# A causal linear attention and feed-forward layer: the last tile's attention within its own slot, and work moved between queues

## The chip, the cores and the metric

The kernel runs on one core of one Trainium2 chip. The metric is the device time of one execution in microseconds (us), the median of several runs. TensorE is called PE below, VectorE DVE, ScalarE ACT, GpSimd POOL and SyncE's queue SP. A change of under 0.2% (4.7 us) is about what a measurement of this kernel can't tell from no change.

## What is computed

The input x is 8 x 2048 x 512 in float32. Per batch, with 16 heads of 32 features and LN for a layernorm without weights:

```python
q, k, v = heads(x @ Wq.T + bq), heads(x @ Wk.T + bk), heads(x @ Wv.T + bv)
q, k = exp(q), exp(k)
kv = cumsum(k[:, :, :, None] * v[:, :, None, :], axis=1)
k1 = cumsum(k, axis=1)
out = einsum('zsD,zsDd->zsd', q, kv) / sum(q * k1, axis=-1, keepdims=True)
x = LN(x + out @ Wo.T + bo)
x = LN(x + tanh(((x @ weight) @ aux_weight1) @ aux_weight2 + bias))
```

## The kernel before

The 2048 rows of each of the 8 batches are cut into 16 tiles of 128 rows, so there are 128 tiles. They are taken in an order in which neighbours belong to different batches: tile n is rows of batch n % 8. The weights are multiplied together and split once at the start, each into a high part (H, fp32r) and a rest (L), and a product of two such matrices takes three passes: H by H, L by H, H by L, over four blocks of 128 rows (`three_pass`, lines 312 to 314, 12 matmuls of 128x512).

All five engines run the same slots, one function `slot(c, k)` each, and slot k works on several tiles at once. The conditions `att` (tile k exists), `prev` (tile k - 1), `ffn` (tile k - 2), `fin` (tile k - 3) and `proj` (tile k + 4) say what is there. So a tile is spread over slots:

- Four slots or more ahead: its rows x are loaded (SP, L277), turned (DVE, L674), split (ACT L567, POOL L761), and Q and K are projected for four tiles at once (PE).
- Slot n: scores of tile n (PE, L410), copied from PSUM into A (ACT, L532), masked (POOL, L723); the running sum of K (DVE, L654) and its product with Q (L662); V projected (PE) and copied out (ACT, L562); the residual's rows loaded (SP, L296) and cbc, the bias after Wo, added to them on POOL (L754).
- Slot n + 1: denominators (PE, L393), the part from the state (L397), and A by V, called AV here (L419). Then o: a reciprocal (DVE, L684), a product (L686), oH (ACT, L542), oL (POOL, L734), the projection by Wo (PE), the sum with the residual (DVE, L700), the first layernorm's statistics (L702 and L704, POOL L765 to L770).
- Slot n + 2: x1, the first layernorm's result (ACT, L522), goes to DRAM and back (SP, L267 and L284) and is turned (DVE, L696) and split (ACT L546, POOL L748); the product with Wf (PE).
- Slot n + 3: bias (DVE, L648), tanh (ACT, L527), the sum with x1 (POOL, L730), statistics (DVE L689 and L692, POOL L738 to L743), the last scaling (ACT, L557), and the store (SP, L300).

Within a slot PE's order is: denominators and state part of tile k - 1, scores of tile k, AV of tile k - 1, state update, Q and K projections, V projection of tile k, Wo for tile k - 1, Wf for tile k - 2. The last slots are cut down: Q and K projections stop after slot 123; slots 124 to 127 are the last with scores, slot 128 has AV, Wo (tile 127) and Wf (tile 126), slot 129 has Wf (tile 127), and slot 130 only finishes tile 127.

Nothing is scheduled by a tool: the order on each engine is the order in which the functions are written, and each queue is taken strictly in order. The PSUM tile ND holds numerators and denominators, one set for all tiles, so those of the next tile can't be written until L686 has read the last ones (semaphore `o_ready`). The SBUF tiles o, oH and oL have one copy each too, as x1s, x1H and x1L. SC is shared: Wo's result lies in its fourth bank, V's in its third, and Q's and Wf's in its first.

```python
                if prev:
                    wait(dve, oproj_done, c.count(k))
                    wait(dve, xb_ready, c.count(k))
                    nc.vector.tensor_tensor(r, oproj_ps, r, ALU.add).then_inc(r_ready, 1)
```

These lines end DVE's slot (L697 to L700). `xb_ready` says that the residual has had its cbc added.

Of the kernel before, what the change touches and what calls it, by code (L numbers as in the profile page):

```python
# [26 lines left out]
def linear_attention_ffn_kernel(nc, x, wqT, wkT, wvT, woT, bq, bk, bv, bo, w, a1T, a2, bf, out):  # L27
    F32 = mybir.dt.float32
    F32R = mybir.dt.float32r
    ALU = mybir.AluOpType  # L30
# [26 lines left out]
    with ctx:  # L57
# [171 lines left out]
        def _(sp):  # L229
# [33 lines left out]
            def slot(c, k):  # L263
# [8 lines left out]
                if c.exists(k + 9):  # L272
                    n = k + 9

                    wait_before(sp, (xl_ready, c.count(n - 1)))
                    for j in range(HG):
                        sp.dma_start(xin[j * HD:(j + 1) * HD, n % XIN, :].rearrange("p (t f) -> p t f", t=HG),  # L277
                                     x_b[n % B, c.it + n // B, j]).then_inc(xin_loaded[n % B], 16)
# [7 lines left out]
                if c.updates_state(k - 1):  # L286
                    n = k - 1
                    wait_before(sp, (k_stored[n % B], c.dma_count(n)), (state_done, c.count(n)))
                    for j in range(HG):
                        sp.dma_start(Ktok[j * HD:(j + 1) * HD, :].rearrange("p (a c) -> p a c", a=HG),  # L290
                                     k_blocks[j]).then_inc(ktok_loaded[n % B], 16)
                if c.exists(k):
# [15 lines left out]
        def _(pe):  # L308
# [40 lines left out]
            def slot(c, k):  # L349
# [4 lines left out]
                pcols = slice((k - 1) % QUAD * P, ((k - 1) % QUAD + 1) * P)  # L354
                ps = ((k - 1) // QUAD) % 2
# [5 lines left out]
                         for g in range(NK) for j in range(HG)]  # L361

# [25 lines left out]
                if prev:  # L388

                    wait_before(pe, (qk1_ready, c.count(k)), (o_ready, c.count(k - 1)),  # L390
                                (state_ready, c.state_count(k - 2)))
                    for g, j, quarter, h in heads:
                        last = nc.tensor.matmul(den_ps[quarter, j, :], ones[h, :], qk1[h, g, :], start=True, stop=True)  # L393
                    last.then_inc(den_done, 1)
                    if c.reads_state(k - 1):
                        for g, j, quarter, h in heads:
                            nc.tensor.matmul(num_ps[quarter, j, :], state[h, (k - 1) % B, g, :], QT[h, ps, g, pcols],  # L397
                                             start=True, stop=False, skip_group_check=True)
# [14 lines left out]
                if prev:  # L413
                    wait(pe, v_ready, c.count(k))
                    wait(pe, masked, c.count(k))
                    for j in range(HG):
                        for g in range(NK):
# [392 lines left out]
```

## Time and profile before

| | us |
|---|---|
| median of 3 runs | 2340.22 |
| lowest and highest | 2339.27 and 2342.91 |
| the profiled execution's own time | 2341.11 |
| its span (first to last instruction) | 2339.2 |
| PE busy in the span | 2249.3 (96%) |
| DVE, ACT, POOL busy | 1494.7, 1004.2, 1415.9 |

The profile is of one execution. Its own time is 1.9 us longer than its span, and 0.9 us longer than the median. In rows of a timeline or a chain the first number is the start in us from the start of the span, and the second the duration in us. Matmuls overlap, so that a row's duration of 0.39 is longer than the step from one to the next, 0.23 at the full clock.

### The profile page before, as it was taken

Reading aid. Unit: us, or ns where it says so; the run is one execution under the profiler, and the core shown is the slowest. Engines: PE = TensorE matmul, PEld = TensorE weight load, DVE = VectorE, ACT = ScalarE, POOL = GpSimd, SP = SyncE. Lnnn points to the kernel's source line nnn. Section 1 sums busy time; section 2 is a strip of 40 time slices with the busy share of each in tenths; the row PEclk is TensorE's granted clock in tenths of the full one; section 3 lists DMA queues with packets and bytes.
Section 4 is the critical chain, followed back from the end, with each engine's and each line's share of the span. In section 5 each row is a group of like instructions: output and inputs, shape, how many; then the busy total and the mean of one; then the engine's idle time right before and its main releaser. Section 6 shows DMA issues by size and latency. Waiting matters only on the chain.

```text
span 2339.2 us, 71230 instructions
## 1 busy us (share of the span) xinstructions
PE 2249.3 (96%) x27784; PEld 1834.5 (78%) x27784; DVE 1494.7 (64%) x2316; ACT 1004.2 (43%) x1683; POOL 1415.9 (61%) x1925
## 2 busy tenths in 40 slices
PE   3999999999999999999999999999999999999985
PEld 2778888888888888888888888888888888878863
DVE  3466676666666766666667666676676666666653
ACT  2344444444444444444444444444444444444432
POOL 1256666666666666666666666666666666666563
PEclk9999999999999999999999999999999999999997
DMA  5133333333333333333333333333333333333221
GB/s 155 48 96 112 107 109 111 103 110 109 106 113 100 113 110 101 110 109 106 113 101 110 114 100 113 106 108 111 103 110 111 101 114 105 107 108 101 71 67 50
DMA packets 294452, 242.73 MB, mean 104 GB/s; under 512 B 33328, under 2 KB 225840, under 8 KB 294192
## 3 DMA queue, kind: packets, MB, share of 16 engines
q1 hardware_dynamic: 294192, 238.69, 32.6%
q8 instruction: 234, 3.83, 0.7%
q14 instruction: 26, 0.21, 0.0%
HBM read 139.99 MB, written 98.57 MB: 102 GB/s over the span
## 4 chain that ended last, share of the span: by engine, by line
PE 92%; DVE 2%; issue 2%; SPq 1%; DMA 1%; ACT 1%; POOL 1%; POOLq 0%; DVEq 0%; ACTq 0%
PE SC L312 25%; PE SC L313 24%; PE SC L314 24%; PE SC L410 6%; PE ND L419 5%; PE ND L397 3%; PE ND L393 2%; PE ND L429 2%; DVE o L684 1%; SPq L277 1%; DMA xres<-x 0%; PE ND L312 0%; PE ND L314 0%; DVE WK L654 0%; PE ND L313 0%
## 5 line engine op out<-in xcount | busy, mean ns | idle before, releaser
L723 POOL TENSOR_SCALAR_AFFINE_SELECT A<-A 128x512 f32<-128x512 f32 x512 | 329.3, 678 | 297.3 <-ACT A L532 297.2
L684 DVE RECIPROCAL o<-ND 128x512 f32<-128x512 f32 x128 | 427.8, 3342 | 1.6 <-PE ND L419 1.3
L700 DVE TENSOR_TENSOR xres<-SC,xres 128x512 f32<-128x512 f32 x128 | 88.5, 692 | 483.2 <-PE SC L314 358.0
L734 POOL TENSOR_TENSOR oL<-o,oH 128x512 fp32r<-128x512 f32 x128 | 165.3, 1291 | 325.0 <-ACT oH L542 325.0
L522 ACT ACTIVATE WK<-xres,shift,rstd 128x512 f32<-128x512 f32 x128 | 104.1, 813 | 501.5 <-POOL shift L770 501.5
L532 ACT ACTIVATE A<-SC 128x512 f32<-128x512 f32 x512 | 264.3, 602 | 36.0 <-PE SC L410 35.0
L312 PE MATMUL SC<-xTH,WqH 128*128 128x512 f32 x512 | 211.1, 412 | 32.3 <-POOL xTL L761 27.6
L312 PE MATMUL SC<-WoH,oH 128*128 128x512 f32 x512 | 202.4, 395 | 17.8 <-issue 16.5
L761 POOL TENSOR_TENSOR xTL<-xin,xTH 128x512 fp32r<-128x512 f32 x128 | 165.6, 1294 | 85.9 <-ACT xTH L567 85.9
L654 DVE TENSOR_TENSOR_SCAN WK<-ones,k,KT 128x128 f32<-128x128 f32 x512 | 207.6, 467 | 8.8 <-PE ND L393 8.3
L312 PE MATMUL SC<-WfH,x1H 128*128 128x512 f32 x512 | 201.0, 393 | 10.4 <-POOL x1L L748 9.4
L312 PE MATMUL SC<-xTH,WkH 128*128 128x512 f32 x512 | 199.9, 390 | 7.2 <-DVE WkL L596 7.2
L537 ACT ACTIVATE QT<-SC,bcol 128x512 f32<-128x512 f32 x128 | 88.3, 690 | 272.3 <-PE SC L314 272.3
L312 PE MATMUL SC<-WvH,xTH 128*128 128x512 f32 x512 | 199.6, 390 | 2.7 <-ACT A L532 2.7
L314 PE MATMUL SC<-WoH,oL 128*128 128x512 f32 x512 | 202.0, 394 | 0.0
L313 PE MATMUL SC<-WoL,oH 128*128 128x512 f32 x512 | 201.8, 394 | 0.0
L313 PE MATMUL SC<-xTL,WqH 128*128 128x512 f32 x512 | 200.8, 392 | 0.7 <-issue 0.3
L314 PE MATMUL SC<-xTH,WqL 128*128 128x512 f32 x512 | 201.4, 393 | 0.0
L313 PE MATMUL SC<-WfL,x1H 128*128 128x512 f32 x512 | 200.4, 391 | 0.0
L314 PE MATMUL SC<-WfH,x1L 128*128 128x512 f32 x512 | 199.9, 390 | 0.0
L313 PE MATMUL SC<-xTL,WkH 128*128 128x512 f32 x512 | 199.7, 390 | 0.0
L314 PE MATMUL SC<-xTH,WkL 128*128 128x512 f32 x512 | 199.6, 390 | 0.0
(100 smaller groups left out, 5006.0 us busy)
## 6 DMA issues: line engine op xcount, KB each, us to landing
xin<-x SPq DMA_DIRECT2D x512, 64.0 KB, 2.0
xres<-x SPq DMA_DIRECT2D x128, 256.0 KB, 2.6
x_rows<-WK SPq DMA_DIRECT2D x128, 256.0 KB, 2.6
WK<-x_rows SPq DMA_DIRECT2D x512, 64.0 KB, 1.9
out<-WK SPq DMA_DIRECT2D x128, 256.0 KB, 2.0
k_rows<-WK SPq DMA_DIRECT2D x120, 256.0 KB, 2.0
WK<-k_rows SPq DMA_DIRECT2D x480, 64.0 KB, 1.9
QT<-wqT SPq DMA_DIRECT2D x4, 256.0 KB, 4.8
```

Source lines behind the costliest of these rows:

```text
L312: nc.tensor.matmul(out, statH(k), movH(k), start=(k == 0), stop=False)
L313: nc.tensor.matmul(out, statH(k), movL(k), start=False, stop=False)
L314: last = nc.tensor.matmul(out, statL(k), movH(k), start=False, stop=(k == NK - 1))
L410: last = nc.tensor.matmul(SC[:, j, g * P:(g + 1) * P], KT[h, s, g, cols], QT[h, s, g, cols], start=True, stop=True)
L419: last = nc.tensor.matmul(num_ps[g * HD:(g + 1) * HD, j, :], V[:, (k - 1) % 2, f0:f0 + HD], A[:, (k - 1) % 2, j, g, :], start=not c.reads_ ...
L522: nc.scalar.activation(x1[:, n % 2, :], xres[:, n % 2, :], ACT.Identity, bias=shift[:, 0:1], scale=rstd[:, 0:1]).then_inc(x1_ready, 1)
L532: nc.scalar.activation(A[:, k % 2, j, :, :].rearrange("p g q -> p (g q)"), SC[:, j, :], ACT.Copy).then_inc(scores_out[j], 1)
L654: last = nc.vector.tensor_tensor_scan(qk1[:, g, :], ones[:, 0:1].to_broadcast([P, P]), KT[:, s, g, cols], k1[:, k % B, g:g + 1], ALU.mult, ...
L684: nc.vector.reciprocal(o[:, :, :], den_ps).then_inc(recip_ready, 1)
L723: last = nc.gpsimd.affine_select(out=A[:, k % 2, j, :, :], in_=A[:, k % 2, j, :, :], compare_op=ALU.is_ge, fill=0.0, base=0, pattern=[[0, ...
L734: nc.gpsimd.tensor_tensor(oL[:, :, :], o[:, :, :], oH[:, :, :].bitcast(F32), ALU.subtract).then_inc(ol_ready, 1)
L761: nc.gpsimd.tensor_tensor(halves[1], xin[:, m % XIN, :].rearrange("p (t g q) -> p g t q", t=HG, q=HD), halves[0].bitcast(F32), ALU.subtrac ...
```

## The change

On PE, DVE, ACT and POOL the steps of AV and o become functions of a tile number (`denominators`, `attend`, `normalise`, `split_o`, `rest_of_o`). They are called as before where tile k exists, and in the slot of the last tile (127) a second time, for tile 127 itself, so that slot 128 no longer has them. Besides:

- ACT copies V (`copy_v`) ahead of `split_o` where `proj` is false (slots 124 to 127); elsewhere it stays behind K's exponential. The last scaling of tile k - 3 moves behind the copy of V and the split of x.
- The addition of cbc to the residual moves from POOL to DVE, from the slot of tile k into that of tile k + 1, just ahead of the sum that uses it.
- SP issues the loads of x for tile k + 9 behind the two loads back from DRAM (x1 and K), not ahead of them.

```diff
@@ sync, slot
-                if c.exists(k + 9):
-                    n = k + 9
-
-                    wait_before(sp, (xl_ready, c.count(n - 1)))
-                    for j in range(HG):
-                        sp.dma_start(xin[...] ...)
                 if c.exists(k - 2):
...
                         sp.dma_start(Ktok[j * HD:(j + 1) * HD, :].rearrange("p (a c) -> p a c", a=HG),
                                      k_blocks[j]).then_inc(ktok_loaded[n % B], 16)
+                if c.exists(k + 9):
+                    n = k + 9
+
+                    wait_before(sp, (xl_ready, c.count(n - 1)))
+                    for j in range(HG):
+                        sp.dma_start(xin[...] ...)
@@ tensor, slot
+                def denominators(n):
+
+                    ts, tcols = (n // QUAD) % 2, slice(n % QUAD * P, (n % QUAD + 1) * P)
+
+                    wait_before(pe, (qk1_ready, c.count(n + 1)), (o_ready, c.count(n)),
+                                (state_ready, c.state_count(n - 1)))
...
+                def attend(n):
+                    wait(pe, v_ready, c.count(n + 1))
+                    wait(pe, masked, c.count(n + 1))
...
-                if prev:
...
+                if att and prev:
+                    denominators(k - 1)
                 if att:
...
-                if prev:
...
+                if att and prev:
+                    attend(k - 1)
...
                     three_pass(v_ps, ...).then_inc(v_done, 1)
+                if att and not c.exists(k + 1):
+                    denominators(k)
+                    attend(k)
                 if prev:
                     output_projection()
@@ scalar, slot
+                def split_o(n):
+                    wait(act, o_ready, c.count(n + 1))
+                    wait(act, oproj_done, c.count(n))
+                    nc.scalar.activation(oH[:, :, :], o[:, :, :], ACT.Copy).then_inc(oh_ready, 1)
+
+                def copy_v():
+                    wait(act, v_done, c.count(k + 1))
+                    wait(act, state_done, c.state_count(k - 1))
+                    nc.scalar.activation(V[:, k % 2, :], v_ps, ACT.Copy).then_inc(v_ready, 1)
...
-                if prev:
...
+                if att and not proj:
+                    copy_v()
+                if att and prev:
+                    split_o(k - 1)
...
-                if fin:
...
-                if att:
...
+                if att and proj:
+                    copy_v()
                 if c.exists(k + 8):
...
+                if fin:
...
+                if att and not c.exists(k + 1):
+                    split_o(k)
@@ vector, slot
+                def normalise(n):
+
+                    wait(dve, num_done, c.count(n + 1))
+                    wait(dve, oh_ready, c.count(n))
+                    wait(dve, ol_ready, c.count(n))
+                    nc.vector.reciprocal(o[:, :, :], den_ps).then_inc(recip_ready, 1)
...
-                if prev:
...
+                if att and prev:
+                    normalise(k - 1)
...
                     nc.vector.transpose(x1s[:, :], x1s[:, :]).then_inc(x1_turned, 1)
+                if att and not c.exists(k + 1):
+                    normalise(k)
                 if prev:
+                    wait(dve, xres_loaded[(k - 1) % B], c.dma_count(k - 1))
+                    nc.vector.tensor_tensor(r, r, cbc[:, :], ALU.add).then_inc(xb_ready, 1)
                     wait(dve, oproj_done, c.count(k))
@@ gpsimd, slot
-                if att:
-                    if not prev:
-                        pool.wait_ge(c_ready, 1)
-                    wait(pool, xres_loaded[k], c.dma_count(k))
-                    nc.gpsimd.tensor_tensor(xres[:, k % 2, :], xres[:, k % 2, :], cbc[:, :],
-                                            ALU.add).then_inc(xb_ready, 1)
...
+                if att and not c.exists(k + 1):
+                    rest_of_o(k)
                 if prev:
                     wait_before(pool, (stats1_ready, c.count(k)))
```

The engine orders at the places that matter. On PE, at the end of slot 127, before (L312 to L314 with Wv are V's projection, with Wo the output projection of tile 126):

```order
L312 MATMUL SC<-WvH,xTH 128x512
L313 MATMUL SC<-WvL,xTH 128x512
L314 MATMUL SC<-WvH,xTL 128x512
L312 MATMUL SC<-WoH,oH 128x512
L313 MATMUL SC<-WoL,oH 128x512
```

and in the changed kernel (L368, L372 and L381 are denominators, state part and AV, of tile 127):

```order
L312 MATMUL SC<-WvH,xTH 128x512
L313 MATMUL SC<-WvL,xTH 128x512
L314 MATMUL SC<-WvH,xTL 128x512
L368 MATMUL ND<-WK,ones 32x128 x16
L372 MATMUL ND<-QT,state 32x128 x16
L381 MATMUL ND<-A,V 32x128 x16
L312 MATMUL SC<-WoH,oH 128x512
L313 MATMUL SC<-WoL,oH 128x512
```

The 48 small matmuls of tile 127 stood behind the Wf product of slot 127, at the head of slot 128; they now stand ahead of Wo for tile 126.

On DVE, from the reciprocal of tile 126 in slot 127 to the first row of slot 128, before:

```order
L684 RECIPROCAL o<-ND 128x512
L686 TENSOR_TENSOR o<-ND,o 128x512
L689 BN_STATS bnst<-WK 128x6
L692 BN_AGGR mv2<-bnst 128x2
L696 STREAM_TRANSPOSE WK<-WK 128x512
L700 TENSOR_TENSOR xres<-SC,xres 128x512
L702 BN_STATS bnst<-xres 128x6
L704 BN_AGGR mv1<-bnst 128x2
L648 TENSOR_TENSOR WK<-SC,bfbc 128x512
```

and in the changed kernel:

```order
L670 RECIPROCAL o<-ND 128x512
L672 TENSOR_TENSOR o<-ND,o 128x512
L712 BN_STATS bnst<-WK 128x6
L715 BN_AGGR mv2<-bnst 128x2
L719 STREAM_TRANSPOSE WK<-WK 128x512
L670 RECIPROCAL o<-ND 128x512
L672 TENSOR_TENSOR o<-ND,o 128x512
L724 TENSOR_TENSOR xres<-xres,cbc 128x512
L727 TENSOR_TENSOR xres<-SC,xres 128x512
L729 BN_STATS bnst<-xres 128x6
L731 BN_AGGR mv1<-bnst 128x2
L677 TENSOR_TENSOR WK<-SC,bfbc 128x512
```

A second reciprocal and product (tile 127) and the cbc addition now stand ahead of the sum for tile 126 (L700 before, L727 now).

On ACT, slot 127 before, from the copies of the scores on:

```order
L532 ACTIVATE A<-SC 128x512 x4
L542 ACTIVATE oH<-o 128x512
L546 ACTIVATE x1H<-WK 128x512
L557 ACTIVATE WK<-WK,shift,rstd 128x512
L562 ACTIVATE V<-SC 128x512
L522 ACTIVATE WK<-xres,shift,rstd 128x512
```

and in the changed kernel:

```order
L552 ACTIVATE A<-SC 128x512 x4
L536 ACTIVATE V<-SC 128x512
L531 ACTIVATE oH<-o 128x512
L566 ACTIVATE x1H<-WK 128x512
L587 ACTIVATE WK<-WK,shift,rstd 128x512
L531 ACTIVATE oH<-o 128x512
L542 ACTIVATE WK<-xres,shift,rstd 128x512
```

The copy of V went from the end of the slot to a place ahead of oH, and oH of tile 127 closes the slot.

## Rows read from the trace of the kernel before

**Rows 1.** Busy time by stretch; after the engines: granted clock, DMA share, GB/s.
```profile
200.00:1200.00 1000.00, 997.52 (x12712) 817.13 (x12711) 666.58 (x1041) 443.64 (x751) 639.65 (x866) 1.00 0.34 108
1200.00:2200.00 1000.00, 994.98 (x12613) 814.29 (x12613) 657.96 (x1031) 441.23 (x745) 634.62 (x863) 1.00 0.34 106
```

**Rows 2.** Chain that ended last: first rows of slots 125, 126, 127; two more of 127.
```profile
2250.56 0.43 PE ND L393 x32
...
2265.63 0.43 PE ND L393 x32
...
2282.31 0.43 PE ND L393 x32
2282.74 0.57 PE ND L397 x24
...
2284.57 1.05 PE ND L419 x32
```

**Rows 3.** Timeline of PE: V's last matmul, Wo's first, in slots 127 and 128.
```profile
2288.88 0.39 PE L314 MATMUL SC<-WvH,xTL 128*128 128x512 f32 x1
...
2291.83 0.47 PE L312 MATMUL SC<-WoH,oH 128*128 128x512 f32 x1 [2.57 <-issue]
...
2307.40 0.77 PE L312 MATMUL SC<-WoH,oH 128*128 128x512 f32 x1 [6.26 <-issue]
```

**Rows 4.** Busy time by stretch, for the clock (the last value but two), slots 126 and 128.
```profile
2275.60:2278.90 3.30, 3.30 (x9) 2.57 (x8) 0.00 (x0) 1.30 (x2) 3.02 (x4) 0.51 0.21 79
...
2306.30:2313.00 6.70, 5.60 (x13) 4.51 (x14) 0.56 (x2) 1.44 (x2) 3.29 (x5) 0.50 0.11 40
```

**Rows 5.** Groups by line, DVE, whole span: busy, mean ns, idle before and its releasers.
```profile
L700 DVE TENSOR_TENSOR xres<-SC,xres 128x512 f32<-128x512 f32 x128 | 88.5, 692 | 483.2 <-PE SC L314 358.0 <-POOL xres L754 125.2
L662 DVE TENSOR_TENSOR WK<-WK,QT 128x512 f32<-128x512 f32 x128 | 89.0, 695 | 4.4
```

**Rows 6.** Timeline of SP and DVE in one steady slot and the next one's L674.
```profile
1196.01 2.63 SPq L277 DMA_DIRECT2D xin<-x  x4
...
1200.65 1.79 SPq L290 DMA_DIRECT2D WK<-k_rows  x4
...
1212.81 0.67 DVE L674 STREAM_TRANSPOSE xin<-xin 128x512 f32<-128x512 f32 x1
```

**Rows 7.** Timeline of DVE, slots 127 to 130.
```profile
2289.03 0.69 DVE L686 TENSOR_TENSOR o<-ND,o 128x512 f32<-128x512 f32 x1
...
2296.45 0.69 DVE L700 TENSOR_TENSOR xres<-SC,xres 128x512 f32<-128x512 f32 x1 [5.26 <-PE SC L314]
...
2301.21 3.36 DVE L684 RECIPROCAL o<-ND 128x512 f32<-128x512 f32 x1 [1.35 <-PE ND L419]
...
2312.90 0.69 DVE L700 TENSOR_TENSOR xres<-SC,xres 128x512 f32<-128x512 f32 x1 [6.14 <-PE SC L314]
...
2322.33 0.71 DVE L696 STREAM_TRANSPOSE WK<-WK 128x512 f32<-128x512 f32 x1 [2.55 <-DMA WK<-x_rows]
2330.44 0.69 DVE L648 TENSOR_TENSOR WK<-SC,bfbc 128x512 f32<-128x512 f32 x1 [7.40 <-PE SC L314]
...
2333.95 0.18 DVE L692 BATCH_NORM_AGGREGATE mv<-bnst 128x2 f32<-128x6 f32 x1
```

**Rows 8.** Timeline of ACT, slots 127 and 129.
```profile
2289.76 0.63 ACT L542 ACTIVATE oH<-o 128x512 fp32r<-128x512 f32 x1 [3.07 <-DVE o L686]
...
2293.90 0.58 ACT L562 ACTIVATE V<-SC 128x512 f32<-128x512 f32 x1
...
2316.10 0.81 ACT L522 ACTIVATE WK<-xres,shift,rstd 128x512 f32<-128x512 f32 x1 [6.55 <-POOL shift L770]
```

**Rows 9.** The chain from x1's rest (tile 127) on; its POOLq row ends POOL's last statistics.
```profile
2323.07 0.64 ACT x1H L546
2323.79 1.27 POOL x1L L748
2325.15 0.77 PE SC L312
...
2335.30 0.32 POOLq L57
```

More of the change, by code:

```diff
@@ L361, in slot @@
                          for g in range(NK) for j in range(HG)]
+                def denominators(n):
+                    ts, tcols = (n // QUAD) % 2, slice(n % QUAD * P, (n % QUAD + 1) * P)
+                    wait_before(pe, (qk1_ready, c.count(n + 1)), (o_ready, c.count(n)),
+                                (state_ready, c.state_count(n - 1)))
+                    for g, j, quarter, h in heads:
+                        last = nc.tensor.matmul(den_ps[quarter, j, :], ones[h, :], qk1[h, g, :], start=True, stop=True)
+                    last.then_inc(den_done, 1)
+                    if c.reads_state(n):
+                        for g, j, quarter, h in heads:
+                            nc.tensor.matmul(num_ps[quarter, j, :], state[h, n % B, g, :], QT[h, ts, g, tcols],
+                                             start=True, stop=False, skip_group_check=True)
+                def attend(n):
+                    wait(pe, v_ready, c.count(n + 1))
+                    wait(pe, masked, c.count(n + 1))
+                    for j in range(HG):
+                        for g in range(NK):
+                            f0 = g * P + j * HD
+                            last = nc.tensor.matmul(num_ps[g * HD:(g + 1) * HD, j, :], V[:, n % 2, f0:f0 + HD],
+                                                    A[:, n % 2, j, g, :], start=not c.reads_state(n),
+                                                    stop=True, skip_group_check=True)
+                    last.then_inc(num_done, 1)
                 def output_projection():
@@ L412, in slot @@
                     last.then_inc(scores_done, 1)
-                if prev:
[L414 to L417, printed above, removed]
-                            f0 = g * P + j * HD
-                            last = nc.tensor.matmul(num_ps[g * HD:(g + 1) * HD, j, :], V[:, (k - 1) % 2, f0:f0 + HD],
-                                                    A[:, (k - 1) % 2, j, g, :], start=not c.reads_state(k - 1),
-                                                    stop=True, skip_group_check=True)
-                    last.then_inc(num_done, 1)
+                if att and prev:
+                    attend(k - 1)
                 if c.updates_state(k - 2):
@@ L538, in slot @@
                                          bias=bcol[:, 0, b:b + 1]).then_inc(q_ready, 1)
-                if prev:
-                    wait(act, o_ready, c.count(k))
-                    wait(act, oproj_done, c.count(k - 1))
-                    nc.scalar.activation(oH[:, :, :], o[:, :, :], ACT.Copy).then_inc(oh_ready, 1)
+                if att and not proj:
+                    copy_v()
+                if att and prev:
+                    split_o(k - 1)
                 if ffn:
```

46 lines of the change are left out of this document (15 added, 31 removed).

## The prediction

> **What bounds the kernel now.** I read the stretches first. In 200 to 2200 us PE is busy 997.5 and 995.0 of each 1000 us, at the full clock (1.00, that is 2.4 GHz) [rows 1]. PE alone sets the pace there: what happens beside it on DVE, ACT, POOL or SP is worth nothing as long as PE doesn't wait. Whatever the change brings must therefore come from the last slots (124 on), where Q's and K's projections are gone.
>
> There I read the chain that ended last. Slot 125 lasts 2265.63 - 2250.56 = 15.07 us, slot 126 lasts 16.68 [rows 2]. The chain runs in each through AV, the reciprocal and product that make o, oH, oL, and Wo. The PE timeline shows the wait: in slot 127 V's last matmul ends at 2288.88 + 0.39 = 2289.27, and Wo starts at 2291.83 after 2.57 us idle; in slot 128 Wo starts after 6.26 us idle [rows 3]. Slot 126 is 1.6 us longer than 125 because the granted clock was 0.51 (the lower level, 1.2 GHz) from 2275.6 to 2278.9, after PE's idle time; slot 125 had the same idle time ahead of Wo and kept the full clock. In slot 128 the clock was 0.50 over the whole of Wo [rows 4].
>
> Last I read the end, tile 127 alone: sum with the residual (L700) at 2312.90, x1 on ACT at 2316.10, x1 back from DRAM and turned at 2322.33 [rows 7, 8], Wf at 2325.15 [rows 9], and 2339.2 - 2325.15 = 14.05 us from there to the end of the span.
>
> **The steady slots: nothing.** Four edits act in them.
> - The cbc addition on DVE: 128 x 0.69 us (the price of L662, whose inputs also both lie in SBUF) = 88 us more on DVE. It stands right ahead of L700, before which DVE sat idle 483.2 us over 128 slots, 3.8 each [rows 5]. It is hidden by that wait; without the cover it would cost up to 0.69 per slot. The residual's load was issued in the slot before, so its new wait is met.
> - POOL loses the same addition. POOL isn't waited for by PE in steady slots: nothing.
> - SP: four loads of x (2.63 us to issue from 1196.01) move behind the loads back of x1 and K, the last of which is issued until 1202.44. They would then be issued by about 1205, and are not needed until DVE turns them at 1212.81 [rows 6]. With some 2 us to land, 5 to 6 us are left. The load of the residual, behind them, stays where it was in the queue.
> - The last scaling behind V's copy and x's split on ACT: the store starts some 1 to 2 us later, with a whole slot in hand.
>
> The rows don't show the other end of these four: a queue that reaches PE after all. I keep -1 (fewer short hiccups) to +2 us for them.
>
> **V's copy ahead of oH, slots 124 to 126.** oH started at 2289.76 in slot 127. V's last matmul ends at 2289.27, so a copy of 0.58 us [rows 3, 8] runs to about 2289.9 and oH starts some 0.1 us later than before. In 124 to 126 the timings repeat within 0.1 us, and this lies on the chain: 3 x 0.07 = +0.2 us. The gain of this edit is in slot 127, below: without it V would wait for o.
>
> **The last tile.** I keep the times of before for slot 127 (start 2282.31) and go step by step.
> 1. o of tile 126 is ready at 2289.03 + 0.69 = 2289.72 [rows 7]. PE may then write ND: 0.1 us to start, then denominators 0.43, state part 0.57, AV 1.05 [rows 2]: done at 2291.9. Wo for tile 126 started at 2291.83, so these 2.05 us fill what was idle, and Wo isn't later.
> 2. DVE: reciprocal 3.36, product 0.69: tile 127's o at 2296.0 (3.36 as in rows 7). Then the cbc addition 0.69, so the sum L700 for tile 126 starts at 2296.6. It was at 2296.45 [rows 7]: +0.15. Here the second reciprocal ends last, not Wo.
> 3. From L700 to x1 on ACT took 3.20 (2312.90 to 2316.10), from there to x1s turned 6.23 (to 2322.33) [rows 7, 8]. So x1 of tile 126 at 2299.8, its x1s back at 2306.05. Meanwhile oH (0.63) and oL (1.27, as the same operation on x1 in [rows 9]) of tile 127 follow its product, with 0.2 for the handovers: ready at 2298.1, and Wo runs for it until 2300.9 (or 2303.3 at half clock): hidden by the wait for x1s, which stands ahead of tile 127's sum on DVE.
> 4. Turning 0.65, cbc 0.69: L700 for tile 127 at 2307.4. It was at 2312.90: **-5.5 us**.
> 5. x1 of tile 127 at 2310.6, back at 2316.85. But DVE must first do tile 126's last statistics. Its Wf starts 2.82 us after x1s (2322.33 to 2325.15), at 2308.9. PE has been idle for long again, and I give it the half clock as in slot 128, where Wo took from 2307.40 to 2312.90, 5.5 us: until 2314.4. From L648 to the end of L692 took 3.69 (2330.44 to 2334.13) [rows 7]: DVE is free at 2318.1, 1.25 us after x1 has landed.
> 6. oH's like for x1 ends at 2319.5. POOL's statistics of tile 126 end 1.67 us after the aggregation's start at 2317.9 (2333.95 to 2335.62): 2319.6. The rest x1L 1.27 and 0.1 to PE [rows 7, 9]: Wf for tile 127 at **2320.95**. It was at 2325.15: -4.2 us. The 14.05 us behind it don't change.
>
> Sum: -4.2 + 0.2 = **-4.0 us**. Against the profiled execution's own 2341.11 that gives 2337.1. That execution lies 0.9 above the median of the runs shown. I put half of this down to slow stretches of the clock that a median run lacks before and after alike, and predict 2336.7, 3.5 us (0.15%) under the median.
>
> **A rule on the clock.** The rows show the same idle time once with and once without a fall of the clock (slots 125 and 126). TensorE: Matmul & The Clock Gate of the Trainium skill (What's actually happening) says that the hardware's observation of activity is not restarted with the kernel, so where the clock changes varies from run to run. This trace agrees in that much. By the rule slot 127's slow stretch isn't always there in the kernel before; I had it in both. In the changed kernel it costs nothing, since step 2 doesn't wait for Wo.
>
> **The rivals.**
> - *More comes off.* A run whose slots 124 to 126 have no slow stretch saves 1.6 per slot, and with a full clock in step 5 tile 126's statistics are done in time, -1.25. For it: the profiled run had such stretches in most of these slots, with the same idle time as the one that had none. Against: nothing in the change makes them rarer there. Time: 2336.7 - 1.25 - 1.6 = 2333.8. Chance 0.27.
> - *The gain is eaten.* Before, slot 127 has no slow stretch in a median run (1.6 less to win), or slot 125 gets one: 2336.7 + 1.6 to + 3.2 = 2338.3 to 2339.9. That the change does not do what it says belongs here: if AV of 127 came later than Wo's start (V's copy late, say), Wo and all behind it slip by as much. Chance, with what reaches into "same", 0.16.
> - *Slower: DVE becomes late.* The cbc addition delays L700, then L648, which must read Wf's result before the next scores may overwrite the bank. It decides once DVE has less than 0.69 us idle before L700. The rows show 3.8 on average. If it did, 112 slots x 0.69 = 77 us: 2414. A smaller form: a load of x that comes late in a few slots, some us each; more than 5 us in all would be slower than before, about 2345. Chance 0.05.
>
> **How the numbers follow.** The forecast has 0.52. Its own range is 2335.5 to 2338.5. The range to 2333.5 below takes in most of the first rival; to 2340.5 above it takes in the second. Faster by over 0.2% means under 2335.5: the first rival and a little of the forecast, 0.30. Slower means over 2344.9: 0.05. Within 0.2%: 0.65.
>
> **What would show it.** PE in 200 to 2200 us stays at 99.5% or more, and the mean slot is unchanged; DVE's busy time is up by about 88 us, POOL's down by 166. In slot 127 the small matmuls of tile 127 stand between V and Wo, with Wo at about 9.6 us after the slot's first matmul, as before. The sum for tile 126 starts 14.3 us after it, and tile 127's sum 10.8 us after that one, not 16.45. Wf for tile 127 starts 38.6 us after slot 127's first matmul, not 42.8, and the end is 14 us later. I would be wrong if PE waited in steady slots, or if the sum of tile 127 waited for Wo and not for x1.

## The result, and the profile after: 0.4% slower

| | before | changed |
|---|---|---|
| median of 6 runs each, us | 2340.17 | 2349.29 |
| lowest to highest | 2339.27 to 2342.91 | 2347.19 to 2354.96 |
| ratio, 95% interval | | 1.0040 [1.0027, 1.0052] |
| profiled execution's own time, span | 2341.11, 2339.2 | 2354.96, 2353.2 |

The forecast was 2336.7 with a range to 2340.5. The time lies 8.8 us above that range. The profiled execution is the longest of the six: its span is 14.0 us longer than before, where the medians differ by 9.1, so its trace shows the loss 4.9 us too large.

The page of the changed kernel, span and busy times:

```profile
span 2353.2 us, 71216 instructions
...
PE 2250.8 (96%) x27784; PEld 1833.2 (78%) x27784; DVE 1620.6 (69%) x2444; ACT 1012.5 (43%) x1683; POOL 1289.1 (55%) x1797
```

PE does the same work in the same busy time (2249.3 before) within a span that is 14.0 us longer. DVE is up by 125.9 us where 88 were expected, and POOL down by 126.8 where 166 were.

Busy time by stretch in the changed kernel (columns as in [rows 1]):

```profile
200.00:1200.00 1000.00, 991.28 (x12563) 810.78 (x12562) 715.50 (x1087) 443.92 (x744) 577.78 (x803) 1.00 0.34 107
1200.00:2200.00 1000.00, 986.82 (x12540) 806.91 (x12507) 711.53 (x1082) 441.44 (x740) 572.34 (x797) 1.00 0.34 106
```

Here is the loss: PE idles 8.7 and 13.2 us in the two steady stretches, where it was 2.5 and 5.0 [rows 1]. The clock is 1.00 in both kernels. The waits of PE in 200 to 2200 us say where (line waited, for what, total us, times, longest), first before:

```profile
PE ND L429 <- issue: 3.0, 7, 0.7
...
PE SC L313 <- issue: 0.3, 1, 0.3
```

and in the changed kernel:

```profile
PE SC L313 <- issue: 13.0, 12, 1.5
PE ND L436 <- issue: 2.7, 9, 0.4
```

Twelve stops of 1.1 us on average, all at the same instruction, and for "issue": no other engine is named. A stop counts from the modelled end of the matmul ahead of it. Each engine's program is its first slots, then a loop whose pass is 8 slots (8 to 111), then the last slots. Measured from one slot's first denominator matmul to the next one's, the 104 slots from 8 to 111 took 1800.1 us before and 1819.2 now. The 12 of them that follow a jump back (16, 24, ... 104) took 17.41 us on average and now take 18.87; the other 92 took 17.30 and now 17.31. So 12 x 1.46 = 17.5 of the 19.1 us lie in these 12 slots. Slot 112, the first behind the loop, took 18.35 and now takes 19.02. The loop has 13 passes, so 13 slots (16 to 112) stand behind a pass's end.

The chain at the start of slot 24 of the changed kernel (start, us, what):

```profile
501.02 0.43 PE ND L368 x32
501.46 0.33 PE ND L372 x4
501.79 0.16 issue
501.95 0.50 PE ND L372 x26
502.45 1.12 PE SC L425 x32
503.57 1.01 PE ND L381 x32
504.58 0.29 PE ND L436 x30
504.87 0.43 PE SC L312
505.30 1.23 issue
506.53 0.40 PE SC L313
```

PE runs dry 4.28 us into the slot, after the first matmul of Q's projection. Start to start, 0.72 to 1.97 us lie between this matmul and the next in the 12 slots; before, 0.31 in six of them and 0.46 to 0.75 in the rest, so that a small part of this loss was there already. In slot 24 of before the same place ran through:

```profile
498.69 0.43 PE ND L393 x32
...
501.81 0.29 PE ND L429 x30
502.10 0.43 PE SC L312
502.53 0.23 PE SC L313
```

```profile
q8 instruction: 1, 0.02, 5.0%
q1 hardware_dynamic: 23, 0.01, 3.7%
```

and in the changed kernel in 498.4 to 499.4, from 2.6 us ahead, with no q8 row:

```profile
DMA packets 143, 0.26 MB, mean 262 GB/s; under 512 B 15, under 2 KB 15, under 8 KB 143
...
q1 hardware_dynamic: 143, 0.26, 71.4%
```

The 0.26 MB are the output store. It was issued at 494.48, 4.2 us ahead of the slot, and now at 497.58, 3.4 us ahead. Before, the store's packets ran from 3.28 to 2.48 us ahead of the slot (medians) and the fetch began as they ended; now they start 2.50 ahead, and the fetch falls among them. Over the 13 slots the first fetch comes 2.0 to 2.6 us ahead of the slot before, and takes 0.9 to 1.2 us. Now it comes either 1.2 to 1.7 us ahead (8 slots), or about 2.2 ahead and takes 1.4 to 2.0 (5 slots). The second fetch comes 1.0 to 1.9 us behind the start before, 1.6 to 3.5 now.

The length of a slot behind a jump back follows the end of this second packet. In all sixteen traces of this study (12 such slots each), where it ended by 2.6 us into the slot, the slot took 17.37 us on average; in the 87 slots where it ended later, each further us made the slot 0.98 us longer (correlation over all 192 slots 0.95).

The groups of the changed kernel that bear on it (columns as in [rows 5]):

```profile
L724 DVE TENSOR_TENSOR xres<-xres,cbc 128x512 f32<-128x512 f32 x128 | 147.6, 1153 | 0.0
L727 DVE TENSOR_TENSOR xres<-SC,xres 128x512 f32<-128x512 f32 x128 | 88.6, 692 | 457.0 <-PE SC L314 456.8
L768 POOL TENSOR_SCALAR ve<-mv 128x1 f32<-128x1 f32 x128 | 68.1, 532 | 14.7 <-DVE mv L715 3.5
```

The cbc addition (L724) takes 1153 ns, not 0.69 us: it mostly starts while POOL still computes oL. L727 still has 457.0 us of idle time ahead of it: DVE isn't late. But POOL's one-column operation `ve` (L768), the first step of the last statistics, takes 532 ns. Before it was

```profile
L738 POOL TENSOR_SCALAR ve<-mv 128x1 f32<-128x1 f32 x128 | 29.8, 232 | 15.3 <-DVE mv L692 2.3 <-issue 1.8
```

The 0.30 us more, 128 times, are 38 us: POOL's busy time fell by 126.8 us and not by the addition's 166.

The tail did what was forecast. DVE in slot 127 of the changed kernel, which begins at 2300.77, and tile 127's Wf on PE:

```profile
2310.49 3.36 DVE L670 RECIPROCAL o<-ND 128x512 f32<-128x512 f32 x1 [0.93 <-PE ND L381]
...
2315.27 0.69 DVE L727 TENSOR_TENSOR xres<-SC,xres 128x512 f32<-128x512 f32 x1
...
2326.09 0.69 DVE L727 TENSOR_TENSOR xres<-SC,xres 128x512 f32<-128x512 f32 x1
...
2335.74 0.68 DVE L719 STREAM_TRANSPOSE WK<-WK 128x512 f32<-128x512 f32 x1
```
```profile
2338.63 0.77 PE L312 MATMUL SC<-WfH,x1H 128*128 128x512 f32 x1 [6.54 <-POOL x1L L778]
```

From slot 127's start to the end of the span are 2353.2 - 2300.77 = 52.4 us; before, 2339.2 - 2282.31 = 56.9. That is -4.5 us.

### The profile page after: what moved, and what is told of

Its sections match the earlier page's. It is cut to its first block, busy times and chain, and to the rows that moved or that the text cites. A ratio compares the mean times of both kernels' runs of the same rounds, so it can differ in the third digit from the quotient of the medians.

```text
span 2353.2 us, 71216 instructions
## 1 busy us (share of the span) xinstructions
PE 2250.8 (96%) x27784; PEld 1833.2 (78%) x27784; DVE 1620.6 (69%) x2444; ACT 1012.5 (43%) x1683; POOL 1289.1 (55%) x1797
## 4 chain that ended last, share of the span: by engine, by line
PE 94%; issue 2%; DVE 2%; ACT 1%; DMA 1%; POOL 1%; SPq 0%; POOLq 0%; DVEq 0%; ACTq 0%
PE SC L312 26%; PE SC L313 25%; PE SC L314 24%; PE SC L425 6%; PE ND L381 5%; PE ND L372 3%; PE ND L368 2%; PE ND L436 2%; DVE o L670 0%; PE ND L312 0%; PE ND L313 0%; PE ND L314 0%; DMA KT<-wkT 0%; DMA QT<-wqT 0%; ACT A L552 0%
## 5 line engine op out<-in xcount | busy, mean ns | idle before, releaser
L727 DVE TENSOR_TENSOR xres<-SC,xres 128x512 f32<-128x512 f32 x128 | 88.6, 692 | 457.0 <-PE SC L314 456.8
L312 PE MATMUL SC<-xTH,WqH 128*128 128x512 f32 x512 | 211.3, 413 | 31.4 <-POOL xTL L785 27.3
L312 PE MATMUL SC<-WfH,x1H 128*128 128x512 f32 x512 | 201.4, 393 | 14.4 <-issue 7.8
L683 DVE TENSOR_TENSOR_SCAN WK<-ones,k,KT 128x128 f32<-128x128 f32 x512 | 207.7, 468 | 9.9 <-PE ND L368 9.9
L312 PE MATMUL SC<-WoH,oH 128*128 128x512 f32 x512 | 201.0, 393 | 9.8 <-issue 7.8
L312 PE MATMUL SC<-xTH,WkH 128*128 128x512 f32 x512 | 200.3, 391 | 7.7 <-DVE WkL L616 7.7
L312 PE MATMUL SC<-WvH,xTH 128*128 128x512 f32 x512 | 199.6, 390 | 2.7 <-ACT A L552 2.7
L314 PE MATMUL SC<-xTH,WqL 128*128 128x512 f32 x512 | 201.4, 393 | 0.0
L314 PE MATMUL SC<-WfH,x1L 128*128 128x512 f32 x512 | 200.5, 392 | 0.0
L314 PE MATMUL SC<-WoH,oL 128*128 128x512 f32 x512 | 200.4, 391 | 0.0
L314 PE MATMUL SC<-xTH,WkL 128*128 128x512 f32 x512 | 199.9, 390 | 0.0
```

Source lines behind the costliest of these rows:

```text
L312: nc.tensor.matmul(out, statH(k), movH(k), start=(k == 0), stop=False)
L314: last = nc.tensor.matmul(out, statL(k), movH(k), start=False, stop=(k == NK - 1))
L683: last = nc.vector.tensor_tensor_scan(qk1[:, g, :], ones[:, 0:1].to_broadcast([P, P]), KT[:, s, g, cols], k1[:, k % B, g:g + 1], ALU.mult, ...
```

## The experiments

Theory A said that the later store (the scaling moved on ACT) lets its packets meet PE's instruction fetch. Its rivals: the cbc addition on DVE, SP's order, or the edits of the tail, which change the code that is fetched. In the table "before" is the kernel before, run beside it; "pass" is the mean length of the 12 slots that follow a jump back (16 to 104; 17.41 before, 18.87 in the changed kernel), and "fetch" the usual start of the first fetch against the slot's start, both from that run's trace.

| run | edit | this / before, us | ratio [95%] | pass | fetch |
|---|---|---|---|---|---|
| e1 | changed, scaling back | 2337.40 / 2338.81 | 0.9994 [0.9985, 1.0003] | 17.57 | -2.15 |
| e2 | before + scaling | 2339.59 / 2338.81 | 1.0000 [0.9991, 1.0009] | 17.46 | -2.55 |
| e3 | changed, SP's order back | 2348.55 / 2338.81 | 1.0045 [1.0030, 1.0060] | 17.97 | -2.2 or -1.4 |
| e4 | changed, cbc back on POOL | 2338.91 / 2338.81 | 0.9999 [0.9990, 1.0008] | 17.51 | -2.5 |
| e5 | before + tail and V | 2335.64 / 2340.10 | 0.9979 [0.9970, 0.9988] | 17.34 | -2.45 |
| e6 | changed, store a slot on | 2338.44 / 2340.10 | 0.9996 [0.9987, 1.0006] | 17.44 | -2.2 |
| e7 | before + cbc on DVE | 2343.61 / 2340.10 | 1.0017 [1.0008, 1.0027] | 17.68 | -2.2 |
| e8 | before + cbc and scaling | 2354.67 / 2340.10 | 1.0061 [1.0045, 1.0076] | 18.57 | -2.2 or -1.4 |
| e9 | e5, store a slot on | 2345.47 / 2340.17 | 1.0024 [1.0015, 1.0033] | 17.56 | -2.55 |
| e10 | e5, V's copy last | 2340.65 / 2340.17 | 1.0004 [0.9995, 1.0013] | 17.34 | -2.5 |
| e11 | before + SP's order | 2346.87 / 2340.17 | 1.0032 [1.0020, 1.0044] | 17.48 | -2.4 |
| e12 | e2, cbc also on DVE | 2354.36 / 2339.28 | 1.0062 [1.0045, 1.0078] | 18.35 | -2.2 or -1.4 |
| e13 | e2, no cbc | 2342.83 / 2339.28 | 1.0010 [1.0001, 1.0020] | 17.46 | -2.5 |
| e14 | changed, cbc waits for x1L | 2347.12 / 2340.22 | 1.0031 [1.0019, 1.0044] | 17.93 | -2.5 |

### One part back, one part alone: e1 to e4

e1 undoes the scaling's move in the changed kernel; e2 makes that move alone in the kernel before:

```diff
@@ scalar, slot, of the changed kernel
+                if fin:
+                    n = k - 3
+                    wait(act, shift2_ready, c.count(n + 1))
+                    nc.scalar.activation(y[:, n % 2, :], ...).then_inc(out_ready, 1)
                 if att and proj:
                     copy_v()
...
-                if fin:
...
@@ scalar, slot, of the kernel before (e2)
-                if fin:
...
                 if c.exists(k + 8):
...
+                if fin:
+                    n = k - 3
...
```

> The changed kernel with one edit undone: ACT's last scaling of tile k - 3 again ahead of V's copy in the steady slots, so that the store of the output is issued 4.1 us before the next slot begins and not 3.4. Theory A (the store's packets now meet a fetch of instructions shortly before the loop's jump back, the fetches that follow come 1 us later, and PE runs dry for up to 1.5 us once in 8 slots): the 19 us in slots 8 to 111 are gone, slots with the jump back are 17.3 to 17.6 long, and only the last slots' gain of 4.5 us is left: about 2336. Theory B (SP's new order of the loads does it): about 2349 as in the changed kernel. Theory C (the cbc addition on DVE does it): 2349 as well.

> The kernel before with one part of the change alone: ACT's last scaling behind V's copy and the split of x. Theory A: the whole of the loss and nothing of the gain: slots with the jump back at 18.5 to 19.4 us, 13 to 19 us slower than before, 2353 to 2359. Theories B and C: 2340, as before.

e1 wins 11.9 us over the changed kernel's 2349.29 (10.5 when each is compared with the kernel before run beside it), as A said. e2 is 2339.59, no change at all, where A had 2353 to 2359: **the late store alone costs nothing**. In e2 the store is issued at 496.01, 3.45 us ahead of slot 24 (499.46), as late as in the changed kernel, but the fetch is still at -2.55, just ahead of the store's first packets at -2.5. (Once in the loop, in slot 16, it came at -1.51, and that slot took 18.38 us.) Theory A as it stood fell.

e3 puts the loads of x back ahead of the loads of x1 and K on SP; e4 moves the cbc addition back to POOL:

```diff
@@ sync, slot, of the changed kernel (e3)
                     sp.dma_start(k_rows, KS).then_inc(k_stored[n % B], 16)
+                if c.exists(k + 9):
+                    n = k + 9
...
                 if c.exists(k - 2):
...
-                if c.exists(k + 9):
...
@@ vector, slot, of the changed kernel (e4)
                 if prev:
-                    wait(dve, xres_loaded[(k - 1) % B], c.dma_count(k - 1))
-                    nc.vector.tensor_tensor(r, r, cbc[:, :], ALU.add).then_inc(xb_ready, 1)
@@ gpsimd, slot
+                if att:
...
+                    wait(pool, xres_loaded[k], c.dma_count(k))
+                    nc.gpsimd.tensor_tensor(xres[:, k % 2, :], xres[:, k % 2, :], cbc[:, :],
+                                            ALU.add).then_inc(xb_ready, 1)
```

> The changed kernel with SP's loads of x again ahead of the loads back of x1 and K. Theory A: no change from the changed kernel, about 2349. Theory B: the loss is gone, 2336.

> The changed kernel with the cbc addition back on POOL (DVE 88 us less busy, POOL 166 more). Theory A: about 2349. Theory C: the loss is gone, 2336.

SP's order is not the cause (2348.55). The cbc addition is half of it: without it the kernel is level with before as well (2338.91). Either of the two parts taken out removes most of the loss, so **it takes both**. Not all of it: with the tail's gain of 4.5 us (e5 below) and no other loss, e1 and e4 would lie near 2334.3, and they lie 3.1 and 4.6 above. What is left in them has such prices by itself: cbc on DVE alone 3.5 (e7), SP's order with cbc on POOL 6.7 (e11; in e4's trace PE waits 6.6 us for ACT's copies A, as there).

### The tail alone, and the store moved away: e5, e6

e5 is the kernel before with only the last slots' part and V's copy. e6 leaves the changed kernel as it is and issues the store of a tile one slot later, behind K's store, away from the pass's end:

```diff
@@ tensor, slot, of the kernel before (e5; likewise on the other engines)
+                if att and not c.exists(k + 1):
+                    denominators(k)
+                    attend(k)
@@ scalar, slot (e5)
+                if att and not proj:
+                    copy_v()
+                if att and prev:
+                    split_o(k - 1)
@@ sync, slot, of the changed kernel (e6)
                     sp.dma_start(k_rows, KS).then_inc(k_stored[n % B], 16)
+                if c.exists(k - 4):
+                    n = k - 4
+                    wait_before(sp, (out_ready, c.count(n + 1)))
+                    sp.dma_start(out_t[n % B, c.it + n // B], y[:, n % 2, :]).then_inc(out_stored[n % B], 16)
...
-                if c.exists(k - 3):
...
```

> Only the last slots' part of the change: tile 127's attention in its own slot and V's copy ahead of oH in slots 124 to 127; scaling, cbc and SP's order as in the kernel before. If the steady slots lose by the other parts alone, slots 8 to 111 take 1800 us as before and the last slots win 4.5 us or a little more (cbc is off DVE's path there): 4 to 6 us under the kernel before run beside it. If the last slots' code itself moves the fetches of the loop, the slots with the jump back are longer than 17.6.

> The changed kernel with one thing moved: the store of the output is issued in the next slot behind the store of K's rows (some 4.5 us into it), far from the fetch 2.2 us before the jump back. Theory A2 (the loss is the meeting of the store's packets with a fetch that the cbc edit has made some 0.3 us later): slots with the jump back 17.2 to 17.8, the whole 1800 us in slots 8 to 111, some 13 us under the changed kernel, 2335. If the loss is of the cbc addition on DVE and of the scaling's place on ACT in some other way than by the store: no change, 2349.

e5 is **the best version of this study**, 2335.64: faster than before by 4.5 us, 0.9979 [0.9970, 0.9988], and 1.1 from the forecast for the whole change. e6 is 2338.44, with cbc and scaling as in the changed kernel, and 10.9 us are back, where 13 were expected. With the store gone from there, PE idles 4.6 us of 1800 and not 19.0. The same stretch in e6, then in the changed kernel:

```profile
200.00:2000.00 1800.00, 1795.44 (x22845) 1471.02 (x22844) 1295.34 (x1976) 805.05 (x1351) 1048.38 (x1455) 1.00 0.35 108
```
```profile
200.00:2000.00 1800.00, 1781.01 (x22621) 1456.39 (x22620) 1287.72 (x1957) 797.54 (x1338) 1035.73 (x1440) 1.00 0.34 107
```

### Both parts on the kernel before: e7, e8

```diff
@@ vector, slot, of the kernel before (e7; e8 has the scaling's move as well)
                 if prev:
+                    wait(dve, xres_loaded[(k - 1) % B], c.dma_count(k - 1))
+                    nc.vector.tensor_tensor(r, r, cbc[:, :], ALU.add).then_inc(xb_ready, 1)
@@ gpsimd, slot
-                if att:
...
```

> The kernel before with cbc on DVE alone. Theory A2: the fetch before the jump back comes at 2.2 us before the slot and not 2.5, but the store's packets end about then, so there is little loss: 0 to 4 us over the kernel before. If DVE's load is the cause by itself: 10 us or more over it.

> The kernel before with two parts of the change, cbc on DVE and the scaling behind V's copy; neither the last slots nor SP's order. Theory A2: both are needed and both together are enough: slots with the jump back 18 to 19.4, 8 to 19 us over the kernel before. Otherwise some third part has a share.

The cbc addition on DVE alone costs 3.5 us, the scaling alone 0.8 (not told from nothing), both 14.6. This is the loss without tail, V or SP's order; with e5's -4.5 it gives 2340.17 + 14.6 - 4.5 = 2350.3, against 2349.29. The trace of e8 in slot 31 shows where the two edits touch:

```profile
631.39 0.74 DVE L699 TENSOR_TENSOR xres<-xres,cbc 128x512 f32<-128x512 f32 x1
...
631.67 0.55 POOL L740 TENSOR_SCALAR ve<-mv 128x1 f32<-128x1 f32 x1
```

`ve` falls into the cbc addition and takes 0.55 us where it took 0.23. It heads POOL's queue, and x1L stands behind it. The two meet in every second slot of e8, the last of each pass among them. The branch back comes 3.60 us ahead of the slot in e2, 3.29 in e8 (medians), and the fetch mostly 1.0 to 1.2 us after it, or up to 0.9 later where the store's packets have started. These 0.3 us put the fetch behind the store's first packets.

### More on the tail and the store: e9, e10

e9 is e6's move of the store on e5. e10 is e5 without the edit to V's copy:

```diff
@@ sync, slot, of e5 (e9)
+                if c.exists(k - 4):
+                    n = k - 4
...
                 if c.exists(k + 9):
...
-                if c.exists(k - 3):
...
@@ scalar, slot, of e5 (e10)
-                if att and not proj:
-                    copy_v()
                 if att and prev:
                     split_o(k - 1)
...
-                if att and proj:
+                if att:
                     copy_v()
```

> The last slots' part alone (as e5_tail_alone), and the store of the output in the next slot behind the store of K's rows. If in the kernel before the store's packets, which end as the fetch begins, still cost something at the jumps back (those slots 17.34 us on average against 17.31 for the rest), this wins at most 1 us over e5: 2335 to 2336. If the new place, among the loads of x1 and K, delays other fetches, it loses 1 to 3 us.

> As e5_tail_alone, but V's copy at the end of ACT's slot in 124 to 127 too. My account of slot 127: the copy then follows oH, x1H and the last scaling, 3 to 3.7 us later than ahead of oH; AV of tile 127 and, behind it on PE, Wo of tile 126 wait for it. The gain of 4.5 us shrinks to about 1: 2339. Rival: V's place doesn't matter, since AV of tile 127 waits for o of tile 126 anyway: 2335.6.

e9 loses 9.8 us against e5, where it was expected to win 1 or lose at most 3. The slots inside a pass take 17.37 us, not 17.31: the store's issue on SP pushes the residual's load on (issued 11.3 us into the slot at the median, not 10.8 as in e5), and POOL's cbc addition waits for it (60.5 us in all, 29.2 in e5). e10 is 5.0 us slower than e5: the last tile's AV within its slot gives nothing unless V is copied ahead of o's split.

### SP's order alone: e11

The edit is the sync part of the change and nothing else:

```diff
@@ sync, slot, of the kernel before
-                if c.exists(k + 9):
-                    n = k + 9
...
                 if c.exists(k - 2):
...
+                if c.exists(k + 9):
+                    n = k + 9
...
```

> The kernel before with SP's order alone (loads of x behind the loads back of x1 and K). The store's and the fetch's times near the jump back are then as before, so no change: 2340 within 2 us. A loss of 3 us or more would give the order a share of its own in the steady slots.

Expected at no cost, it costs 6.7 us. The residual's load is behind the moved loads of x, which now follow at once (issued 11.5 us into the slot at the median, 10.6 before). POOL's groups and PE's waits in 200 to 2200 us of e11:

```profile
L754 POOL TENSOR_TENSOR xres<-xres,cbc 128x512 f32<-128x512 f32 x128 | 165.5, 1293 | 101.8 <-DMA xres<-x 101.5
```
```profile
PE SC L312 <- ACT A L532: 8.4, 18, 1.0
```

Before, L754 waited 27.8 us in all, and PE waited for A 3 times, 1.6 us. POOL is held up by the load, so its statistics, ACT's x1 and then ACT's copies of the scores come later, and Q's projection must wait for the bank. With cbc on DVE nothing on POOL waits for that load, and the order is free (e3 against the changed kernel).

### DVE's gain or POOL's loss: e12, e13

e12 keeps cbc on POOL and adds it a second time on DVE, so its output has cbc twice. e13 adds it on neither, so its output lacks the bias behind Wo. Both have the scaling's move.

```diff
@@ vector, slot, of e2 (e12)
                 if prev:
-                    wait(dve, oproj_done, c.count(k))
                     wait(dve, xb_ready, c.count(k))
+                    nc.vector.tensor_tensor(r, r, cbc[:, :], ALU.add).then_inc(xb2_ready, 1)
+                    wait(dve, oproj_done, c.count(k))
+                    wait(dve, xb2_ready, c.count(k))
@@ vector, slot, of e2 (e13)
-                    wait(dve, xb_ready, c.count(k))
+                    wait(dve, xres_loaded[(k - 1) % B], c.dma_count(k - 1))
@@ gpsimd, slot (e13)
-                if att:
...
```

> As e2_scaling_alone (the scaling behind V's copy), with a second addition of cbc on DVE besides POOL's; the output has cbc twice. The fetch before the jump back came 2.5 us before the slot with cbc on POOL and 2.2 with cbc on DVE. If DVE's longer list of instructions is what makes it later, it comes at 2.2 here too, meets the store, and the loss of e8 appears (12 us or more over the kernel before). If POOL's shorter list is the cause: 2.5, and 2340.

> As e2_scaling_alone, with cbc added on neither engine (the output lacks the bias after Wo). If POOL's shorter list makes the fetch later: 2.2, and a loss of 12 us or more. If DVE's longer list does: 2.5, and 2340.

It is the addition on DVE that costs (e12 2354.36, `ve` 403 ns, pass 18.35), not its lack on POOL (e13: `ve` 232 ns, pass 17.46). e13's 3.6 us over its own before aren't in these slots, and I haven't traced them; its profiled execution lies 1.4 us under its median.

### The addition held back: e14

```diff
@@ vector, slot, of the changed kernel
                 if prev:
+                    if att and c.exists(k - 2):
+                        wait(dve, x1l_ready, c.count(k - 1))
                     wait(dve, xres_loaded[(k - 1) % B], c.dma_count(k - 1))
```

> The changed kernel with one more wait: DVE adds cbc only when POOL has written x1L of the same slot (some 4 us before the slot's end, 1.5 us before the sum needs it). Theory A3, the whole chain: beside the cbc addition POOL's first small statistics operation takes 0.53 us and not 0.23; x1L is 0.3 later; PE's sequencer waits for it, jumps back 0.3 later and asks for the fetch 0.3 later, when the store's packets are in the queues. With the wait, the small operation takes 0.23, the addition 0.7 and not 1.15, the fetch comes at -2.5, slots with the jump back take 17.2 to 17.8 and slots 8 to 111 some 1801 us: 2336. If the meeting of POOL and DVE has nothing to do with it: 2349 as in the changed kernel.

```profile
L726 DVE TENSOR_TENSOR xres<-xres,cbc 128x512 f32<-128x512 f32 x128 | 200.4, 1566 | 400.4 <-POOL x1L L780 400.4
...
L770 POOL TENSOR_SCALAR ve<-mv 128x1 f32<-128x1 f32 x128 | 29.7, 232 | 14.6 <-DVE mv L715 3.5
```

`ve` is back at 232 ns, the branch at -3.59 and the fetch at -2.5, and two stops at Q's projection are left of twelve, with the store as late as in the changed kernel (issued at 496.12 for slot 24 at 499.56). That is what the explanation asks for. The chain in six traces, medians over the 13 passes' ends (`ve` is its duration, the rest are starts or, for x1L, the end, in us against the slot's start):

| run | `ve` | x1L written | PE's branch | store's first packet | first fetch |
|---|---|---|---|---|---|
| before | 0.23 | -3.87 | -3.61 | -3.28 | -2.48 |
| e2 | 0.23 | -3.87 | -3.60 | -2.51 | -2.52 |
| e1 | 0.54 | -3.54 | -3.28 | -2.94 | -2.16 |
| e8 | 0.55 | -3.55 | -3.29 | -2.51 | -1.56 |
| changed | 0.55 | -3.55 | -3.28 | -2.50 | -1.53 |
| e14 | 0.23 | -3.87 | -3.59 | -2.50 | -2.52 |

But little time came of it (2347.12, where 2336 was expected). Slots 8 to 111 take 1806.4 us in the trace, 12.8 under the changed kernel's and 6.3 over before. The addition now lies beside POOL's split of x and takes 1566 ns, Wf's result is read later (L677), and the next scores wait for its bank. This shows only behind a jump back, where most slots take 17.8 us; the others take 17.29. The chain of e14 in slot 24:

```profile
499.99 0.57 PE ND L372 x24
500.56 0.47 issue
501.03 1.17 PE SC L425 x32
```

L677 runs from 500.13 to 500.82 there. Slot 116 besides takes 22.54 us in this execution, about 5 more than its like: the chain puts 2.65 us of "issue" on DVE ahead of its running sum (L683), and PE stops for 3.5 us. Why DVE stopped isn't known.

## Why the prediction was wrong

**The step that failed is "The steady slots: nothing"**, with its bound of -1 to +2 us for four edits. By the medians the sum is +9.1 us, of which -4.5 is the tail, so the four edits cost 13.6. The reasons on cbc and on the scaling each left something out, and most of the loss needs both; the one on POOL was wrong too, and the one on SP's order holds only with cbc on DVE.

- *"It is hidden by that wait"* (cbc on DVE, 0.69 per slot). The cover held: L727 still has 3.6 us of idle time ahead of it per slot. But I asked only who waits for DVE, and not what POOL runs at that moment. The addition takes 1153 ns, and it holds up the `ve` that starts beside it, from 0.23 to 0.55 us. The row that priced it, L662, could have warned: in 102 of the 104 slots of the loop it ran beside POOL's mask (L723). It started first and paid nothing, and that mask took 0.81 us on average, where the others took 0.63. Before, in slot 8 (two masks in one row):

```profile
224.88 0.69 DVE L662 TENSOR_TENSOR WK<-WK,QT 128x512 f32<-128x512 f32 x1
```
```profile
225.26 1.41 POOL L723 TENSOR_SCALAR_AFFINE_SELECT A<-A 128x512 f32<-128x512 f32 x2 [2.40 <-ACT A L532]
```

- *SP's order*: right for the changed kernel (e3), wrong as a general step: the sentence that the residual's load "stayed where it was in the queue" looked at the order and not at the time. With cbc on POOL it costs 6.7 us (e11).

**The rival for "slower"** named DVE becoming late, priced 2414 or 2345, chance 0.05. The sign was right and the mechanism wrong. It left no room for a DMA that meets another, and 0.05 was too little for four edits whose far end no row showed, as the prediction itself says.

**The tail was right.** Sum for tile 126 at +14.5 us into slot 127 (forecast 14.3), tile 127's sum 10.82 later (10.8), Wf for tile 127 at +37.9 (38.6), end 14.6 behind it (14), -4.5 in all (-4.2). The last two misses, 0.7 early and 0.5 late, nearly cancel, which is luck; the first is there because Wf for tile 126 ran at half clock only in part. As in step 5, tile 127's x1s (2335.74) is turned directly behind tile 126's last statistics, so these and not the transfer end last. e5 measures this part by itself at 2335.64 against 2340.10; e10 confirms that V's copy ahead of oH is needed for it.

**What stays open.** That the fetch behind the store costs PE time some four us later rests on the times of the packets in sixteen traces, and on e1, e4, e6, e8 and e14, which take one link away or put it in. Which code each of the three packets carries the trace doesn't say; that the first is PE's is inferred, since it follows PE's branch, mostly by 1.0 to 1.2 us, in every run, and moves with it. e3 is as slow as the changed kernel at the median, though its slots behind a jump back take 17.97 us and not 18.87: its profiled execution is the shortest of four and the changed kernel's the longest of six. Of e7's 3.5 us, 12 x 0.27 = 3.2 lie in the slots behind a jump back, two of which have the second packet nearly as late as in the changed kernel (ended 3.6 us into the slot): probably the same collision, seldom. e13's 3.6 were not followed further.

## What to carry to other kernels

Work on an idle engine is not free because nobody waits for that engine: price an added VectorE operation with two SBUF inputs by what GpSimd runs at that moment, and follow GpSimd's next results. In a kernel whose TensorE is 99.5% busy, look at the instruction queue in the DMA view around each jump of a loop, and try large stores a few us away from it; the new place has its own price (e9 lost 9.8 us by it). Edits that cost little by themselves (0.8 and 3.5 us here) can cost 14.6 together, so time a bundle's parts and pairs; here the part worth keeping was e5.

## What the runs showed of the hardware

- A POOL operation on 128x1 took 0.23 us alone, and 0.55 on average wherever it met DVE's addition of two 128x512 SBUF tiles (103 of the loop's 104 slots in the changed kernel, 51 in e8, which makes the averages 532 and 395 ns). That addition took 0.65 us alone, 1153 ns on average in the changed kernel, where it mostly starts beside oL, and 1566 in e14 beside POOL's split of x. The timeline of the changed kernel in slot 126:

```profile
2293.00 0.95 DVE L724 TENSOR_TENSOR xres<-xres,cbc 128x512 f32<-128x512 f32 x1
...
2293.49 0.54 POOL L768 TENSOR_SCALAR ve<-mv 128x1 f32<-128x1 f32 x1
```

- The slow clock of the prediction's step 5 was there in the Wf product of tile 126, in part: 0.62 on average from 2327.5 to 2332.0, with the last four of its twelve matmuls at full speed, where the whole of Wo in slot 128 had 0.50 before [rows 4].
